# A decoder layer on one core: masks ahead of inversions, moved rotations, and a second stage with plain low rank and a longer pipeline

## What is computed

```
x = layernorm(x + attention(x))     # 32 query heads, 8 key/value heads of 32, rotary, causal
x = layernorm(x + conv(x, ctx))     # features*similarity, 3 taps, weight 128 x 128 x 3
x = layernorm(x + ffn(x))           # 8 experts, rank 16, softmax gates
```

```
low = x A^T (8 x 16);  scores = 8 softmax(x Wr^T + br);  out = 2 * sum_h scores_h * (low_h B_h^T)
```

## Time and profile before

| What | Value |
|---|---|
| Median of 3 runs | 1571.94 us |
| The profiled execution: its own time | 1568.54 us |
| Its span (first to last instruction) | 1566.8 us |
| Mean granted TensorE clock (1 is full) | 0.981 |
| TensorE matmul busy, share of the span | 1402.8 us, 90% |
| VectorE | 1215.3 us, 78% |
| ScalarE | 859.7 us, 55% |
| GpSimd | 969.3 us, 62% |
| DMA moved | 213.03 MB |

### The profile page before, as it was taken

The page is one execution under the profiler, slowest core; times in us unless marked ns, Lnnn a source line. Parts: engine busy times, 40 slices in busy tenths (PEclk is TensorE's granted clock), DMA queues, the critical chain, the costliest instruction groups (busy, mean ns, idle before and its releaser), DMA issues. The chain is left out here.

```text
span 1566.8 us, 32397 instructions
## 1 busy us (share of the span) xinstructions
PE 1402.8 (90%) x8288; PEld 1051.4 (67%) x8288; DVE 1215.3 (78%) x4094; ACT 859.7 (55%) x3196; POOL 969.3 (62%) x873
## 2 busy tenths in 40 slices
PE   6899898999999898999985899999999999999985
PEld 4566666666666666666662677777777777777774
DVE  5777677776777677776776588888888888888886
ACT  5777777777777777777775233333333333333332
POOL 3766666666666666666664566656666666666652
PEclk9999999999999999999997999999999999999996
DMA  6343434444443434344456765565555655556541
GB/s 223 106 135 108 131 113 132 113 132 121 123 134 108 132 112 132 115 135 120 121 171 181 188 147 148 156 156 134 145 141 147 161 139 143 145 141 155 147 108 41
DMA packets 109005, 213.03 MB, mean 136 GB/s; under 512 B 26656, under 2 KB 32288, under 8 KB 108960
## 3 DMA queue, kind: packets, MB, share of 16 engines
q1 hardware_dynamic: 108960, 212.51, 49.0%
HBM read 131.83 MB, written 34.47 MB: 106 GB/s over the span
## 5 line engine op out<-in xcount | busy, mean ns | idle before, releaser
L439 PE MATMUL wo_ps<-weights,halves 128*128 128x512 f32 x2304 | 572.2, 400 | 12.1 <-DVE weights L617 12.1
L701 ACT ACTIVATE pexp<-sm,smin 128x128 f32<-128x128 f32 x1024 | 398.5, 391 | 209.0 <-DVE smin L568 168.8
L439 PEld LDWEIGHTS wo_ps<-weights,halves 128*128 128x128 f32 x2304 | 422.7, 189 | 128.9 <-issue 34.6
L1050 PE MATMUL wo_ps<-weights,halves 128*128 128x512 f32 x1488 | 398.6, 401 | 2.0 <-DVE yz L1152 2.0
L1421 POOL TENSOR_TENSOR prods<-prod,prods 128x512 fp32r<-128x512 f32 x192 | 267.0, 1392 | 197.7 <-ACT prods L1333 196.7
L821 POOL TENSOR_TENSOR pn<-pexp,prec 128x512 f32<-128x512 f32 x256 | 267.3, 1044 | 180.4 <-DVE prec L575 180.4
L1050 PEld LDWEIGHTS wo_ps<-weights,halves 128*128 128x128 f32 x1488 | 273.5, 190 | 60.0 <-issue 3.7
L1333 ACT CAST prods<-prod 128x512 fp32r<-128x512 f32 x192 | 118.7, 619 | 326.8 <-DVE prod L1192 318.7
L568 DVE CUSTOM_DVE_ANT_0 sm<-s_ps,mask_t 128x128 f32<-128x128 f32 x1024 | 237.4, 288 | 14.7 <-PE s_ps L469 5.1
L1061 PE MATMUL conv_ps<-prods,weights 128*128 128x512 f32 x576 | 174.7, 412 | 41.2 <-POOL prods L1421 39.8
L575 DVE RECIPROCAL prec<-psum_row 128x4 f32<-128x4 f32 x256 | 44.8, 175 | 201.3 <-ACT pexp L701 201.1
(11 more groups left out here) (103 smaller groups left out, 1732.7 us busy)
## 6 DMA issues: line engine op xcount, KB each, us to landing
att<-sim_scratch SPq DMA_DIRECT2D x192, 252.0 KB
pt<-blocks SPq DMA_DIRECT2D x640, 64.0 KB, 2.0
ctx_t<-in_ctx SPq DMA_DIRECT2D x32, 576.0 KB, 4.7
raw<-in_xT SPq DMA_DIRECT2D x32, 512.0 KB, 3.6
raw<-ot_scratch SPq DMA_DIRECT2D x32, 512.0 KB, 6.5
xn<-in_x SPq DMA_DIRECT2D x32, 512.0 KB, 7.2
out<-late SPq DMA_DIRECT2D x32, 512.0 KB, 3.0
ot_scratch<-ot SPq DMA_DIRECT2D x63, 256.0 KB, 2.1
```

The lines of the kernel that those rows point to most:

```text
L439: mm = pe.matmul(qkv_ps[(par + g) % 2][:], xs[:, par, xl, k], w_sb[:, wl, g, k], start=(k == 0 and n == 0), stop=(k == KT - 1 and n == 2))
L701: ins = nc.scalar.activation(pexp[:, c % 2, i * P:(i + 1) * P], sm[:, c % 2, i * P:(i + 1) * P], ACT.Exp, bias=smin[:, c % 2, i:i + 1], sc ...
L1050: mm = pe.matmul(wo_ps[n][:], os_t[:, par, ol, k], wo_sb[:, wl, k, n * BANK:(n + 1) * BANK], start=(k == 0 and m == 0), stop=(k == KT - 1 ...
```

## The change

**First stage.** On VectorE the mask of a chunk now precedes the inversion of the chunk before it. The rotation of query group 2 moves to the head of the step, ahead of the last chunk's inversion and the first mask; that of group 1 from the end of chunk 5's work to its front. On TensorE the turn of the second query half and the first weighing move from slot 7 to 9, the second weighing and the keys' turn from 15 to 17. ScalarE copies the second query half at chunk 3, not 2; GpSimd adds it at chunk 0, not 1, and the first half at chunk 5, not 6.

**Second stage.** The rank reduction takes x2 and A, Wr as plain float32 (8 matmuls of 136 columns, not 16 rounded ones of 272); `low_x2` and the two instructions that put the parts together go. The weights wa come by one DMA at the head of the second stage, and no longer by two pieces split in the first. Both remaining normalisations move from VectorE to ScalarE, as res = rstd * y + shift, with shift = -mean * rstd made by VectorE and GpSimd. Turning and expanding the low rank of a sequence move into the next step (slots 1 and 3), the turns of x2 to slots 11 and 12, the reduction to 14, the convolutions to other slots. VectorE's, ScalarE's and GpSimd's orders follow: on ScalarE `high_lt(z)` and `normalise1(c)` stand behind `high_o`, `normalise2(f)` behind the second product, `normalise3(z)` behind the third, ahead of the copies of x2; on GpSimd the root of z stands behind the second product's remainder and `low_o`'s second half behind the third's. The steps after the loop are written in the new order too.

```diff
-    wo_sb, wa_sb, wb_sb, wx_sb = later_weights(weights)
-    LATER = KT + 3
+    wo_sb, wb_sb, wx_sb = later_weights(weights)
+    LATER = KT + 2
     BY_POOL = (1, 4, 8, 9)
...
-                    if s == 7:
+                    if s == 9:
                         turn_q(a, 1)
                 if valid(b):
-                    if s == 7:
+                    if s == 9:
                         weigh(b, par, 0)
-                    if s == 15:
+                    if s == 17:
                         weigh(b, par, 1)
                 if valid(t):
-                    if s == 15:
+                    if s == 17:
                         turn_k(t)
                     if s == 22:
                         turn_q(t, 0)
...
+                if p == 0 and valid(a):
+                    rotate(a, 1 - par, 2)
+                if p == 0 and valid(b):
+                    invert(b, NC - 1)
+                if p == 5 and valid(t):
+                    rotate(t, par, 1)
+                if valid(a):
+                    mask_min(a, p)
                 if p > 0 and valid(a):
                     invert(a, p - 1)
-                if p == 0 and valid(b):
-                    invert(b, NC - 1)
-                if valid(a):
-                    mask_min(a, p)
                 if at_step(t, 1) and p == 0:
                     sum_neighbours(0)
                 if p == 3 and valid(t):
                     turn_p(b, NC - BEHIND + p)
                 if p >= BEHIND and valid(a):
                     turn_p(a, p - BEHIND)
-                if p == 0 and valid(a):
-                    rotate(a, 1 - par, 2)
                 if p == 2 and valid(t):
                     rotate(t, par, 0)
-                if p == 5 and valid(t):
-                    rotate(t, par, 1)
...
-                if p == 2 and valid(a):
+                if p == 3 and valid(a):
                     copy_q(a, 1)
...
-                if p == 6 and valid(t):
+                if p == 5 and valid(t):
                     add_q(t, par, 0)
+                if p == 0 and valid(a):
+                    add_q(a, 1 - par, 1)
                 if p == 0 and valid(b):
                     scale(b, NC - 1)
-                if p == 1 and valid(a):
-                    add_q(a, 1 - par, 1)
                 if p > 0 and valid(a):
...
-    xt = sb("xt", [P, 2, KT, S], F32R)
+    xt = sb("xt", [P, KT, S])
+    wa_t = sb("wa_t", [P, KT * LOWW])
...
-    CONV_AT = (8, 10, 12, 14, 15, 17)
-    FIRST_CONV_AT = (11, 13, 15, 17, 18, 20)
-    LOWCHAIN = 4
+    CONV_AT = (9, 11, 13, 15, 17, 20)
+    FIRST_CONV_AT = (11, 13, 15, 17, 19, 20)
+    LOWCHAIN = 2
...
+        sp.dma_start(wa_t[:], wa).then_inc(consts_in, 16)
...
-            wait(pe, xt_lo, after(t, 2, 2))
+            wait(pe, xt_in, after(t, 2, 2))
             for k in range(KT):
-                for xl in range(2):
-                    mm = pe.matmul(ffn_place(t)[0][:, 0:2 * LOWW], xt[:, xl, k],
-                                   wa_sb[:, k].rearrange("p l n -> p (l n)"),
-                                   start=(k == 0 and xl == 0), stop=(k == KT - 1 and xl == 1))
+                mm = pe.matmul(ffn_place(t)[0][:, 0:LOWW], xt[:, k], wa_t[:, k * LOWW:(k + 1) * LOWW],
+                               start=(k == 0), stop=(k == KT - 1))
...
-                if valid(z) and s == 2:
-                    expand(z)
+                if valid(z):
+                    if s == 1:
+                        turn_low(z)
+                    if s == 3:
+                        expand(z)
                 if valid(f):
-                    if s in (9, 10):
-                        turn_x2(f, par, s - 9)
-                    if s == 13:
+                    if s in (11, 12):
+                        turn_x2(f, par, s - 11)
+                    if s == 14:
                         reduce_rank(f)
-                    if s == 15:
-                        turn_low(f)
...
+                wait(dve, normed[1], after(t - 1, 1, 1))
...
-        def normalise(t, par, n):
-            src = yz[:, n]
-            dst = (x1[:, par, 1:D + 1], x2[:, par])[n]
-            wait(dve, rstd_done[n], after(t, 1, 1))
-            dve.tensor_scalar(dst, src, mv[n][:, 0:1], rstd[n][:], ALU.subtract, ALU.mult).then_inc(normed[n], 1)
...
-        def low_x2(t, n):
-            wait(dve, xt_hi, after(t, 2, n + 1))
-            dst = xt[:, :, n * NJ:(n + 1) * NJ].rearrange("p l t s -> p l (t s)")
-            dve.tensor_tensor(dst[:, 1], ffn_place(t)[n][:], dst[:, 0].bitcast(F32), ALU.subtract).then_inc(xt_lo, 1)
...
-            dve.tensor_copy(lowhi[:], ffn_place(t)[0][:, LOWW:2 * LOWW]).then_inc(low_step, 1)
+            dve.tensor_tensor(logit[:], ffn_place(t)[0][:, HR:LOWW], br_t[:], ALU.add).then_inc(low_step, 1)
             dve.wait_ge(low_step, after(t, LOWCHAIN, 1))
-            dve.tensor_tensor(low[:], ffn_place(t)[0][:, 0:LOWW], lowhi[:], ALU.add).then_inc(low_step, 1)
-            dve.wait_ge(low_step, after(t, LOWCHAIN, 2))
-            dve.tensor_tensor(logit[:], low[:, HR:LOWW], br_t[:], ALU.add).then_inc(low_step, 1)
-            dve.wait_ge(low_step, after(t, LOWCHAIN, 3))
             dve.tensor_reduce(nmax[:], logit[:], AX.X, ALU.max, negate=True).then_inc(gate_in, 1)
         def gate_low(t):
...
                 average(c, 0)
+            if valid(z):
+                low_lt(z)
+                add(z, 1 - par, 2, 0)
+                add(z, 1 - par, 2, 1)
+            if valid(c):
+                multiply(c, 1 - par, 0)
             if valid(f):
                 add(f, par, 1, 1)
-            if valid(c):
-                normalise(c, 1 - par, 0)
-                multiply(c, 1 - par, 0)
-            if valid(f):
                 count(f, 1, 1)
-            if valid(z):
-                add(z, 1 - par, 2, 0)
-            if valid(f):
                 average(f, 1)
+            if valid(c):
+                multiply(c, 1 - par, 1)
             if valid(z):
                 count(z, 2, 0)
-            if valid(c):
-                multiply(c, 1 - par, 1)
-            if valid(f):
-                normalise(f, par, 1)
-            if valid(z):
-                add(z, 1 - par, 2, 1)
                 count(z, 2, 1)
+                average(z, 2)
             if valid(c):
                 multiply(c, 1 - par, 2)
-            if valid(f):
-                low_x2(f, 0)
-            if valid(z):
-                average(z, 2)
-            if valid(f):
-                low_x2(f, 1)
             if valid(t):
                 add(t, par, 0, 0)
+                count(t, 0, 0)
             if valid(c):
                 multiply(c, 1 - par, 3)
-            if valid(t):
-                count(t, 0, 0)
-            if valid(c):
                 multiply(c, 1 - par, 4)
                 add(c, 1 - par, 1, 0)
+                count(c, 1, 0)
             if valid(f):
                 route(f)
             if valid(c):
                 multiply(c, 1 - par, 5)
             if valid(f):
                 gate_low(f)
-            if valid(c):
-                count(c, 1, 0)
-            if valid(f):
-                low_lt(f)
...
+        def normalise1(t, par):
+
+            wait(act, shifted[0], after(t, 1, 1))
+            nc.scalar.activation(x1[:, par, 1:D + 1], yz[:, 0], ACT.Identity, bias=shift[0][:],
+                                 scale=rstd[0][:]).then_inc(normed[0], 1)
+
+        def normalise2(t, par):
+
+            wait(act, shifted[1], after(t, 1, 1))
+            nc.scalar.activation(x2[:, par], yz[:, 1], ACT.Identity, bias=shift[1][:],
+                                 scale=rstd[1][:]).then_inc(normed[1], 1)
+
...
-            nc.scalar.copy(xt[:, 0, n * NJ:(n + 1) * NJ].rearrange("p t s -> p (t s)"),
-                           ffn_place(t)[n][:]).then_inc(xt_hi, 1)
+            nc.scalar.copy(xt[:, n * NJ:(n + 1) * NJ].rearrange("p t s -> p (t s)"),
+                           ffn_place(t)[n][:]).then_inc(xt_in, 1)
...
-            if n == 2:
-                pool.wait_ge(rstd_done[n], after(t, 1, 1))
-                pool.tensor_tensor(shift3[:], nmean3[:], rstd[n][:], ALU.mult).then_inc(shifted, 1)
+            pool.wait_ge(rstd_done[n], after(t, 1, 1))
+            pool.tensor_tensor(shift[n][:], nmean[n][:], rstd[n][:], ALU.mult).then_inc(shifted[n], 1)
```

121 lines of the change are left out of this document (55 added, 66 removed).

## The result

The changed kernel takes 1470.57 us (median of 4, 1470.43 to 1470.94) against 1572.02 for the kernel before (1571.41 to 1572.42), measured beside it: a ratio of 0.9355, 95% interval 0.9339 to 0.9372, 101 us faster. The prediction was 1515, with a range of 1484 to 1550: the sign and both mechanisms were right, the size was not, and the time lies outside the range. It is rival B's 1470, but only half for B's reason.

A forecast was written before the change was run, and what follows sets the result against it. Both stages looked TensorE-bound with some waits, the first stage's made by a mask, exponentials and inversion relay. 34.5 us (stage 1) plus 22 (stage 2), ends 0, gave 56.5 us off: 1515 us, range 1484 to 1550.

The forecast's parts named there:

- rival B: Both stages run at TensorE's own pace without waits: 102 us less, 1470 us; chance 0.14.
- Stage 1: First stage (attention): period falls from 25.09 to 23.94 us, 34.5 us less over 30 steps.
- The other half: First stage, from score round 0 to score round 1: TensorE's own 11.37 us, with ScalarE's some 11.3 just fitting.
- TensorE's own work: Work without waits: 11.37 and 11.52 us for the first stage's half-steps, 20.09 us a step in the second.
- Rival F: First stage gains nothing, as a wait for the rotation holds the exponentials at every step: 1550 us; chance 0.07.
- 20.09 + 0.35 + 0.1 = 20.54: Second stage's forecast period in us: own work, dearer reduction, tightness; 0.76 less than 21.30, 22 us over 29 periods.
- The reduction: Second stage: 8 plain f32 matmuls take 2.34 us in place of 1.99, +0.35 us a step.
- D: Second stage: weight loads half bare, the reduction costs 3.4 us, 9 us lost there: 1546 us; chance 0.10.
- E: Second stage: weight loads wholly bare (reduction 4.37 us) and convolution waits stay: slower than before, 1606 us; chance 0.05.
- The tightness of 0.1 us: Second stage: 0.1 us a step left over for tightness, with the 1.21 us of waits counted as gone.
- Ends: Parts outside the two stages' periods, such as SP's loads and the tail's two reductions: 0 together, +-4 us.
- C: Second stage keeps its waits and loses 10 us: 1547 us, or 1530 if half the waits go; chance 0.14.

The follow-up runs named there:

- run 4: The changed kernel with the rotation of query group 1 put behind the mask of chunk 5 instead of in front: 1434.18 us.
- runs 7 to 11: run 7, run 8, run 9; the kernel before with only both normalisations moved to ScalarE, 1578.13 us; the changed kernel with the old convolution slots, 1539.8 us.
- run 3: The changed kernel with the plain rank reduction run twice over: 1526.75 us.
- run 7: The kernel before with the plain rank reduction alone, all second-stage orders and slots as they were: 1562.53 us.
- run 8: The changed kernel with the rounded reduction put back, with its split, additions and two weight loads, other orders kept: 1497.64 us.
- run 9: The changed kernel with both normalisations put back on VectorE: 1493.63 us.
- run 2: The changed kernel with the old first-stage order, the second stage all new: 1510.21 us.
- run 6: The kernel before with the new first-stage slots, rotations, copies and additions, but each inversion still ahead of the next mask: 1620.13 us.

## Why the prediction was right in kind and wrong in size

**Stage 1: right.** Forecast 34.5 us, measured 39.2. The half-step after score round 1 was laid out at 12.57 us and is 12.59 (311.28 to 323.87); the rotation at +3.5 is at +3.48, chunk 5's exponentials at +5.79 are at +5.71, the wait of 1.05 for the copy qt is 1.19, and the turn of xn waits no more. The other half was to be 11.37 and is 11.16: that accounts for nearly all of the 0.20 us a step by which the period came out shorter. TensorE's own work was put too high here as well, by the method that failed in stage 2: without waits run 4 has 11.15 and 11.33 us for the two halves, where 11.37 and 11.52 were taken from the brackets. That it is the rotation which holds the half-step, and not ScalarE's load, was argued there; run 4 shows it. Rival F, where every chunk would be held by it, falls.

**Stage 2: the step that failed.** The mechanism, both waits going with VectorE's shorter queue and the later slots, is what the trace and runs 7 to 11 show. The sum "20.09 + 0.35 + 0.1 = 20.54" is off in every term, all on the same side, against a measured 19.48; the 1.06 us over 29 periods are the 31 us missed there.

- The reduction: I took 2.34 us (+0.35) from the score round; it is 1.85 by run 3 (-0.15; run 7 has -0.16). That is 0.50 x 29 = 14.5 us. The trace of before has streams over row groups and column groups, and either bound lay above the truth: the range of the term, 2.12 to 4.37, did not hold it. The Trainium skill (FP8 and Floating Point Precision, TensorE Precision Notes) has four passes for true FP32, so the columns of the rounded form; by it the term was 1.99, the nearest of the prices I had, and still above what came. Rivals D and E, with bare weight loads, fall: this chip's trace shows nothing of them in 8 matmuls at 1.85 us.
- TensorE's own work: I took 21.30 less the 1.21 us in two brackets, 20.09. It is 19.48 + 0.15 = 19.63 with the old reduction, the same as in run 8 without its wait: 0.46 x 29 = 13 us. Two faults are in the 20.09. The 1.21 us of brackets belong to an even step, whose period is 21.54, and not to the mean of 21.30; put right by itself, this gives a higher figure, 20.33. And the waits of an even step were 21.54 - 19.63 = 1.91 us, not 1.21. A bracket counts from the modelled end of the last matmul, which lies behind the start that a next one could have had (0.38 for 0.54 in run 8, 0.52 for 0.67 in run 9), a gap that is small enough has no bracket at all, and the first matmuls behind a wait take longer (three in 0.80 us, 1215.69 to 1216.49 in the earlier trace rows, where 0.70 is usual).
- The tightness of 0.1 us: 3 us; there is none.

So of 53 us in this stage, some 48 are waits removed (29 x 1.67, the mean of 21.30 less 19.63) and 29 x 0.15 = 4 the shorter reduction.

VectorE was to be busy near 70 of 100 us and is busy 81: it lost some 3 us a step and not 4, since its products became longer (last section), and the step is shorter than forecast.

**Ends: too cautious.** Taken as 0 +- 4, they gave 6. Of these 5.4 are in the tail. I feared the tail's reductions; they take this (TensorE's timeline after), no more than in the loop, where the earlier trace rows had 2.93:

```profile
1444.84 2.01 PE L1073 MATMUL wo_ps<-wa_t,xt 128*128 128x136 f32 x16
...
1453.64 2.02 PE L1073 MATMUL ffn_ps<-wa_t,xt 128*128 128x136 f32 x16
```

Not all of this is the kernel's doing: in run 4, whose second stage is the same, the second of them takes 2.72 us and the tail 46.7 us instead of 45.9.

**The rivals.** B's number was hit by luck, not by its case: it wanted both stages without waits, and the first has its 1.19 us a step. Its 102 us are a sum of waits by brackets, which are too small, and its 1.1 us a step is worked out nowhere: 1.21 less the dearer reduction's 0.35 is 0.86, so B by the prediction's own terms was 95 us, 1477. The full case, as run 4 shows, is 137 us. B had a chance of 0.14, yet the range ended at 1484 and left its number out. C falls, though run 7 is C by construction: it keeps the waits, with the old order and slots.

**Neither part of the second half that was run alone does it.** The plain reduction gives 7 us, the normalisations on ScalarE cost 7; in the full change, to leave out the reduction costs 27, the normalisations 23, the slots 69. The later slots by themselves, the new order of VectorE and the move of the low-rank chain into the next step were not run.

## What to carry to other kernels

Where a pipelined engine seems to wait a little, take its own work from pitches between starts and not as the period less the bracketed idle: the brackets here missed over a third of it (they had 1.21 of 1.91 us in an even step), and a mean period over uneven steps must not be mixed with the brackets of one of them. Put a wait that is only needed later behind the work that feeds the chain; one instruction group on the wrong side of one mask was worth 36 us of 1470. A relief on one engine can be worth little or less than nothing alone (7 and -7 us here), while the whole set is worth 61 us (run 2), so price the set, and then look for the member of the set that costs (here the rotation's move).

## What the runs showed of the hardware that was not expected

Eight plain f32 matmuls of 136 columns over the full array cost 1.85 us (run 3), a little less than 16 rounded ones of 272 columns at 1.99, though both columns times records come to the same if a plain record streams at half the pace: 16 x 136 x 2 = 16 x 272. The 16 weight loads of a plain reduction have a mean of 190 ns in the list of lines (1100 to 1260 us), the rounded ones 188; laid one behind another they would be 3.0 us, so they lie beside the streams and each other as the rounded ones do.

VectorE's and GpSimd's operations on two SBUF inputs can lengthen each other. The page after, costliest groups (columns: busy, mean ns | idle):

```profile
L1177 DVE TENSOR_TENSOR prod<-att,x 128x512 f32<-128x512 f32 x192 | 186.1, 985 | 13.9 <-DMA att<-sim_scratch 11.1
...
L1387 POOL TENSOR_TENSOR rstd<-var,power 128x1 f32<-128x1 f32 x96 | 76.6, 798 | 70.3 <-DVE var L1168 69.0
...
L1381 POOL TENSOR_TENSOR halves<-raw,halves 128x512 fp32r<-128x512 f32 x60 | 90.5, 1509 | 1.4 <-ACT halves L1282 1.4
```

The products had a mean of 831 ns before, the roots 677, and the halves 1337 (list of lines, the whole program); the remainders of products did not become longer (1392 ns before, 1364 after). A product with GpSimd idle takes 0.68 us (1113.36 in the changed kernel); the two started at 1107.88 take 3.03, with GpSimd at work all along (a product's remainder, then from 1108.62 the halves for 1.75). The Trainium skill (GPSIMD Engine Reference, Specifications) has the SBUF interfaces shared with VectorE for instructions with two SBUF inputs; the trace agrees and adds a price, 3.03 / 2 - 0.68 = 0.8 us for each of these two products. It costs nothing here, as TensorE is the bound in this stage.

TensorE's granted clock fell to 0.53 in the 3 us behind a wait of 2.33 us in run 6, though not behind every such wait, and stayed at 1.00 behind waits of 1.3 us in the kernel before, so a longer wait there cost more than itself. What decides it was not run.
